# The down projection's leftover columns accumulated in the banks of the second segment's groups

## The reference, cut to what matters

```python
x = x + (x @ W.T + b + coeff * (x @ (2 * mask - 1)))        # stage 1, 8 x 256 tokens, 1024 wide
gate = x @ W_gate.T + 0.5 * (x @ A_gate[i].T) @ B_gate[i].T # F = 2752, i: adapter of the sequence, rank 16
up   = x @ W_up.T   + 0.5 * (x @ A_up[i].T)   @ B_up[i].T
act  = silu(gate) * up
x    = x + act @ W_down.T + 0.5 * (act @ A_down[i].T) @ B_down[i].T   # the stage of the change
```

## Time and profile before

| | |
|---|---|
| runs, median of 3 | 1665.02 us (1662.74 to 1666.45) |
| the profiled execution | 1666.28 us |
| its span, first to last instruction | 1664.6 us |
| TensorE busy | 1574.9 us (95%) |
| VectorE busy | 1247.0 us (75%) |
| ScalarE busy | 798.7 us (48%) |
| granted TensorE clock, mean | 0.981 |

### The profile page before, as it was taken

One profiled execution on the slowest core, in us unless ns is written; L12 is line 12 of the kernel. 1 busy time (PEld: TensorE's weight loads), 2 busy tenths in 40 slices (PEclk: granted clock), 3 DMA queues, 4 the chain that ended last, 5 costly groups with the idle time before them and its releaser, 6 DMA issues.

```text
span 1664.6 us, 22933 instructions
## 1 busy us (share of the span) xinstructions
PE 1574.9 (95%) x7502; PEld 1318.0 (79%) x7502; DVE 1247.0 (75%) x2168; ACT 798.7 (48%) x1466; POOL 331.7 (20%) x629
## 2 busy tenths in 40 slices
PE   6999958999999999998999769999999999999999
PEld 6999936888888888877888558888888888777887
DVE  7998767766666766679888786666667667698886
ACT  7998644444444444443333354444444444443332
POOL 0100121222222222232410010222222222402210
PEclk9999969999999999999999989999999999999999
DMA  8979572444444444694983643444444444968763
GB/s 328 347 285 309 177 246 86 149 149 149 141 149 138 147 143 142 219 332 162 362 272 106 202 137 114 148 149 149 148 149 149 149 147 144 339 193 283 252 208 117
DMA packets 135813, 321.03 MB, mean 193 GB/s; under 512 B 19344, under 2 KB 42000, under 8 KB 135696
## 3 DMA queue, kind: packets, MB, share of 16 engines
q0 software_dynamic: 55072, 175.81, 31.8%
q1 hardware_dynamic: 76016, 135.37, 24.6%
q10 hardware_dynamic: 4608, 8.39, 1.4%
HBM read 229.32 MB, written 90.18 MB: 192 GB/s over the span
## 4 chain that ended last, share of the span: by engine, by line
PE 84%; DVE 9%; DMA 4%; issue 2%; ACT 1%; SPq 1%; POOL 0%; DVEq 0%; ACTq 0%; POOLq 0%
PE ps L1321 57%; PE ps L1317 24%; DMA fx<-x_scratch 2%; PE ps L1423 2%; DVE acc L958 2%; DVE lo L955 2%; DVE op_b L955 1%; DVE fx L955 1%; DVE raw L955 1%; PE ps L1402 0%; DMA m_raw<-in_mask 0%; DVE m_raw L958 0%; DMA x_in<-in_x 0%; DMA a_in<-in_a_gu 0%; ACT hi L650 0%
## 5 line engine op out<-in xcount | busy, mean ns | idle before, releaser
L1321 PE MATMUL ps<-op_b,hi 128*128 128x512 f32 x1696 | 526.3, 392 | 17.4 <-ACT ps L650 9.8
L955 DVE TENSOR_TENSOR lo<-raw,hi 128x512 fp32r<-128x512 f32 (+2 forms) x646 | 339.0, 532 | 135.1 <-ACT hi L650 132.6
L650 ACT ACTIVATE hi<-raw 128x512 fp32r<-128x512 f32 (+1 forms) x598 | 308.8, 520 | 238.8 <-PE ps L1321 204.6
L1321 PEld LDWEIGHTS ps<-op_b,hi 128*128 128x128 f32 x1696 | 320.0, 189 | 87.6 <-ACT ps L650 10.7
L1321 PE MATMUL ps<-op_b,lo 128*128 128x512 f32 x848 | 332.4, 392 | 0.0
L1321 PE MATMUL ps<-op_d,hi 128*128 128x512 f32 x800 | 250.6, 395 | 11.8 <-DVE acc L958 11.8
L1317 PE MATMUL ps<-op_b,hi 128*128 128x512 f32 x720 | 227.3, 397 | 9.5 <-DVE op_b L955 9.5
L958 DVE TENSOR_TENSOR acc<-acc,ps 128x512 f32<-128x512 f32 x272 | 185.2, 686 | 54.9 <-PE ps L1321 51.5
L533 POOL DMA_DIRECT2D operand_scratch<-ot x140 | 75.6, 540 | 660.4 <-DVE ot L955 625.1
L1321 PEld LDWEIGHTS ps<-op_d,hi 128*128 128x128 f32 x800 | 150.6, 190 | 48.8 <-DVE acc L958 17.1
L1321 PEld LDWEIGHTS ps<-op_b,lo 128*128 128x128 f32 x848 | 160.2, 189 | 34.0
(11 more groups left out here) (123 smaller groups left out, 2204.2 us busy)
## 6 DMA issues: line engine op xcount, KB each, us to landing
operand_scratch<-ot POOLq DMA_DIRECT2D x140, 512.0 KB, 3.9
op_d<-operand_scratch POOLq DMA_DIRECT2D x140, 512.0 KB, 10.7
raw<-in_wgu SPq DMA_DIRECT2D x168, 256.0 KB, 4.2
m_raw<-in_mask SPq DMA_DIRECT2D x64, 512.0 KB, 5.7
raw<-in_wd SPq DMA_DIRECT2D x160, 128.0 KB, 5.0
fx<-x_scratch SPq DMA_DIRECT2D x64, 256.0 KB, 3.8
b_in<-in_b_gu POOLq DMA_DIRECT2D x264, 32.0 KB, 2.3
w_in<-in_w SPq DMA_DIRECT2D x16, 512.0 KB, 5.5
```

Source lines behind the costliest of these rows:

```text
L650: return nc.scalar.activation(o, i, ACT.Copy)
L955: return nc.vector.tensor_tensor(o, a, b, ALU.subtract)
L1321: return mm(dst, weight, v, start=False, stop=stop, skip_group_check=True)
```

## The change

The eight pieces move into segment 1, two into each group: the even one (h = 2 hp) ahead of p7, the odd one ahead of p4. Their halves accumulate onto the group's own banks: the even piece onto y and z, the first-listed half of the odd one into ps6 or ps7, its second half onto x. So p3's add of y comes after the even piece, and of the leftover's adds one a group remains (the bank ps6 or ps7). `bd_in` becomes two slots, each with the adapter rows of one group, in a place of its own; it is loaded four times a block. All of segment 1's operand loads are issued without waiting, and the next block's adapters are loaded after segment 2's operands.

The diff, its core (left out: declarations, `left_bank`, the same change of `bd_in`'s index on VectorE):

```diff
@@ -17,6 +17,7 @@
 SEGS, SEGK = 5, 2
+LEFT_SEG = 1
@@ -65,12 +66,12 @@
     for hp in range(HP):
-        order += [("d", s, seg, hp, u) for u in PRODUCTS[:6]]
-        if seg == 0 and hp == 0:
-            order += [("td", s, PAIRS)]
-        order += [("d", s, seg, hp, u) for u in PRODUCTS[6:]]
-    if seg == 0:
-        order += [("l", s, h) for h in range(HT)]
+        for u in PRODUCTS:
+            if u == "p4" and (seg, hp) == (0, 0):
+                order += [("td", s, PAIRS)]
+            if u in ("p7", "p4") and seg == LEFT_SEG:
+                order += [("l", s, 2 * hp + int(u == "p4"))]
+            order += [("d", s, seg, hp, u)]
     return order
@@ -227,15 +228,14 @@
     with ExitStack() as down:
-        with ExitStack() as before:
-            sb(before, "pad_bd", [P, 40 * 256], f32)
-            bd_in = sb(before, "bd_in", [P, 4, H], f32)
...
+        sb(down, "pad_lw", [P, LW_RING * HALVES, P], f32)
+        bd_in = sb(down, "bd_in", [P, 2, 4, 2 * P], f32)
@@ -520,9 +520,9 @@
                     weight_dma(("d", s, seg, hp), name)
-            if seg == 0:
-                for h in range(HT):
-                    weight_dma(("l", s, h), "a")
+                if seg == LEFT_SEG:
+                    for h in (2 * hp, 2 * hp + 1):
+                        weight_dma(("l", s, h), "a")
@@ -552,12 +552,15 @@
-    def load_b_down(adapter):
+    def load_b_down(adapter, s, hp):
+        if hp > 1:
+            pool.wait_ge(lo_ready, at["l", s, 2 * hp - 3] + 1)
...
-                pool.dma_start(bd_in[r:r + RANK, b, :], b_down[ds(adapter[b], 1), :, :].rearrange(
-                    "a r n -> (a r) n")).then_inc(bd_loaded, 16)
+                pool.dma_start(bd_in[r:r + RANK, hp % 2, b, :],
+                               b_down[ds(adapter[b], 1), :, 2 * P * hp:2 * P * (hp + 1)].rearrange(
+                                   "a r n -> (a r) n")).then_inc(bd_loaded[hp % 2], 16)
@@ -623,26 +626,29 @@
             load_acc(s, h)
-        load_b_down(adapter)
-        for u in ("p1", "p5", "p6", "p3", "p4"):
+        for u in PRODUCTS[:3]:
...
-        pool.wait_ge(lo_ready, at["l", s, HT - 1] + 1)
-        load_operand(s, 1, "p7")
-        load_operand(s, 1, "p2")
-        if s < BLOCKS - 1:
+        load_b_down(adapter, s, 0)
+        for u in PRODUCTS[3:]:
+            load_operand(s, 1, u)
+        load_b_down(adapter, s, 1)
+        for seg in range(2, SEGS):
+            for u in PRODUCTS:
+                pool.wait_ge(pe_done, done["d", s, seg - 2, HP - 1, u])
+                load_operand(s, seg, u)
+                if seg == 2 and u in ("p6", "p7"):
+                    load_b_down(adapter, s, 2 + int(u == "p7"))
+            if seg > 2 or s == BLOCKS - 1:
+                continue
...
+            pool.wait_ge(lo_ready, at["l", s, HT - 1] + 1)
...
-        for seg in range(2, SEGS):
-            for u in PRODUCTS:
-                pool.wait_ge(pe_done, done["d", s, seg - 2, HP - 1, u])
-                load_operand(s, seg, u)
@@ -723,9 +729,10 @@
             _, s, h = key
-            act.wait_ge(bd_loaded, 16 * 8 * (s + 1))
+            hp, cols = h // 2, slice(h % 2 * P, (h % 2 + 1) * P)
+            act.wait_ge(bd_loaded[hp % 2], 16 * 8 * bd_turn(s, hp))
...
-            copy(tile[TR:P, :, :], bd_in[TR:P, :, h * P:(h + 1) * P])
+            copy(tile[TR:P, :, :], bd_in[TR:P, hp % 2, :, cols])
@@ -1033,8 +1040,6 @@
     def make_first(g):
-        if g[0] == "l":
-            return
@@ -1074,7 +1080,7 @@
             sub(slot_ap(lo, key), src, slot_ap(hi, key)).then_inc(lo_ready, 1)
-        if n + 1 < len(plan.items) and plan.group(plan.items[n + 1]) != g:
+        if n + 1 < len(plan.items) and plan.items[n + 1][-1] in ("p1", "q1"):
@@ -1206,22 +1212,20 @@
             dve.wait_ge(acc_loaded[2 * hp + row], 16 * (s + 1))
-        dve.wait_ge(pe_done, done[key])
+        dve.wait_ge(pe_done, done["l", s, 2 * hp] if (seg, u) == (LEFT_SEG, "p3") else done[key])
...
-        if (seg, hp, u) == (1, 0, "p5"):
-            dve.wait_ge(left_added, left_count(s, HT - 1, HALVES - 1))
+        if (seg, u) == (LEFT_SEG + 1, "p5"):
+            dve.wait_ge(left_added, left_count(s, hp))
...
-    def add_left(key):
-        _, s, h = key
-        dve.wait_ge(pe_done, done[key])
-        for half in range(HALVES):
-            dst = acc[:, h, half * N:(half + 1) * N]
-            if h == 0 and half == 0:
-                dve.wait_ge(d_added, d_count(s, 0, HP - 1, "p4"))
-            add(dst, dst, left_bank(h, half)[:, :]).then_inc(left_added, 1)
+    def add_left(s, hp):
+        dve.wait_ge(pe_done, done["l", s, 2 * hp + 1])
+        dve.wait_ge(d_added, d_count(s, LEFT_SEG, hp, "p7"))
+        dst = acc[:, 2 * hp + 1, N:2 * N]
+        add(dst, dst, ps[6 + hp % 2][:, :]).then_inc(left_added, 1)
@@ -1272,10 +1276,14 @@
             evict(key)
-        elif key[0] == "d" and key[4] != "p1":
+        elif key[0] == "d" and key[4] != "p1" and (key[2], key[4]) != (LEFT_SEG, "p3"):
             add_down(key)
         elif key[0] == "l":
-            add_left(key)
+            _, s, h = key
+            if h % 2:
+                add_left(s, h // 2)
+            else:
+                add_down(("d", s, LEFT_SEG, h // 2, "p3"))
         if key[0] == "d" and key[2:] == (0, 0, "p1"):
@@ -1447,8 +1455,6 @@
             pe.wait_ge(c_made, c_count(s, PAIRS, "c12"))
-        if (seg, hp, u) == (1, 0, "p1"):
-            pe.wait_ge(left_added, left_count(s, HT - 2, HALVES - 1))
@@ -1461,29 +1467,29 @@
     def left(s, h):
-        key = ("l", s, h)
+        key, hp = ("l", s, h), h // 2
+        g = (s * SEGS + LEFT_SEG) * HP + hp
+        x_ps, y_ps, z_ps = ps[3 * (g % 2)], ps[3 * (g % 2) + 1], ps[3 * (g % 2) + 2]
...
-            pe.wait_ge(d_added, d_count(s, 0, HP - 2, "p4"))
-        elif h == 1:
-            pe.wait_ge(td_sum, 2 * HALVES * (s + 1))
-        elif h == 2:
-            pe.wait_ge(d_added, d_count(s, 0, HP - 1, "p4"))
-        else:
-            pe.wait_ge(left_added, left_count(s, h - 3, HALVES - 1))
+            pe.wait_ge(td_ready, 2 * HALVES * (s + 1))
...
-        for half in range(HALVES):
-            dst, i = left_bank(h, half), 2 * ot_slot[s, KP, ("b11", "b12")[half]]
-            mm(dst[:, :], high[:, 0:P], ot[:, i, :], start=True, stop=False)
-            mm(dst[:, :], high[:, 0:P], ot[:, i + 1, :], start=False, stop=False)
-            mm(dst[:, :], high[:, 2 * P:3 * P], ot[:, i, :], start=False, stop=False)
-            if h == 0 and half == 0:
-                pe.wait_ge(td_ready, 2 * HALVES * (s + 1))
-            mm(dst[:, :], high[:, P:2 * P], act21[:, half * N:(half + 1) * N], start=False, stop=False)
+        for half, dst in ((1, ps[6 + hp % 2] if h % 2 else y_ps), (0, x_ps if h % 2 else z_ps)):
+            mm_to = mm_new if h % 2 and half else mm_on
+            if h % 2 == 0 and half == 0:
+                pe.wait_ge(d_seeded, g + 1)
+            elif h % 2 and half == 0:
+                pe.wait_ge(d_added, d_count(s, LEFT_SEG, hp, "p7"))
+            elif h % 2 and hp > 1:
+                pe.wait_ge(left_added, left_count(s, hp - 2))
+            i = 2 * ot_slot[s, KP, ("b11", "b12")[half]]
+            mm_to(dst[:, :], high[:, 0:P], ot[:, i, :], start=h % 2 == 1 and half == 1)
+            mm_to(dst[:, :], high[:, 0:P], ot[:, i + 1, :])
+            mm_to(dst[:, :], high[:, 2 * P:3 * P], ot[:, i, :])
+            mm_to(dst[:, :], high[:, P:2 * P], act21[:, half * N:(half + 1) * N])
...
-                end = mm(dst[:, b * S:(b + 1) * S], low[:, v * P:(v + 1) * P], act_t[:, cols], start=False,
-                         stop=b == 1)
+                end = mm_to(dst[:, b * S:(b + 1) * S], low[:, v * P:(v + 1) * P], act_t[:, cols], stop=b == 1)
```

13 lines of the change are left out of this document (7 added, 6 removed).

## The result

The changed kernel took 1652.67 us (median of 4 runs, 1651.78 to 1655.76) against 1664.67 us of the kernel before (4 runs, 1662.74 to 1666.45): ratio 0.9931, 95% interval 0.9914 to 0.9949.

A forecast was written before the change was run, and what follows sets the result against it. VectorE was taken to bound the leftover, TensorE the rest of the down projection. -11.58 + 0.9 = -10.7 us took the profiled 1666.28 to 1655.6; the profiled run being 1.26 above the median, 1654.3 was predicted, range 1651.8 to 1661.3.

The forecast's parts named there:

- the sum's first term: Both blocks, segment 0's last group to segment 2: TensorE's gaps shrink by 5.77 and 5.81 us, together -11.58 us.
- the new wait: Segment 1, odd piece's second half waiting for p7's add, and p3: 0.15 us in 6 groups, 0.9 us; margin 0.14.
- The leftover's gaps: TensorE from segment 0's last group to segment 2: 6.58 us lost per block disappear, 0.81 at p3 remains.
- The term for p3 carried over: Segment 0's last group: p3 still starts late, as one group earlier, costing 0.81 us against 1.85 before.
- The adds: VectorE: 16 leftover adds per block become 4, freeing 7.2 us of VectorE per block, worth nothing by themselves.
- VectorE's queue in a group: Segment 1: VectorE needs 11.6 of 14.2 us per group; p7's add done at 11.3, p5's at 3.7.
- (1): Rival: VectorE's chains in segment 1 overrun in full, 6.9 us instead of 0.9, so 1660.3 us; chance 0.13.
- (2): Rival: VectorE becomes segment 1's bound, 16.7 against 14.2 us a group, 20 us in 8 groups: 1673.5 us; chance 0.05.
- (4): Rival: the gaps only move, 1.4 us in each of eight groups, no change, 1665 us; chance 0.07.
- (3): Rival: GpSimd's adapter issues in segment 1's first two groups hold VectorE, 5.2 us in both blocks: 1659.5 us; chance 0.05.
- Loads and adapters: Operand, b_down and next block's adapter loads, issued at new times, all arrive before they are needed: cost 0.
- One sign of being wrong: The prediction would be wrong if block 1 started later than its 5.8 us earlier.

The follow-up runs named there:

- the run with the first piece late: Kernel before, with the first leftover piece's weights prepared after p5's add of segment 0's last group instead of ahead of it: 1665.02 us, ratio 1.0002.
- the run with four adds in the old place: Kernel before, pieces still between segments 0 and 1, only 4 of 16 leftover adds per block, the other halves left out of the output: 1656.16 us.
- The experiment on the chain: Changed kernel plus two unread VectorE additions after p6's add in segment 1's groups 0 to 2, ahead of p7's add: 1659.61 us, ratio 0.9966.

## Why the prediction was right

**The whole.** The sum was -10.7 us. The two stretches together gave 11.5, the 11.58 of the sum's first term; the 0.9 for the new wait was not lost. That the two profiled executions differ by 10.5, so near to 10.7, is in part luck, since other parts of the program took 1 us back. The medians differ by 12.0.

**The leftover's gaps** (-6.58 + 0.81 per block). Right in cause and size: the stretch came out at 67.23 us, forecast 67.2. That the first piece's weights held up p3 is borne out by the run with the first piece late, where that wait is gone. The term for p3 carried over, 0.81, measured 0.87 and 0.83 (group of 10.39 and 10.35 us). It stayed when the leftover went to segment 2, so the prediction's cause fits, the steps of the adapter's input together with two sums.

**The adds** ("worth nothing by themselves once TensorE is the bound"). Too little said. It did the sum no harm, because the gaps were counted once, but the run with four adds in the old place shows 4.65 us per block from them alone: they would have made TensorE the bound there too. And with the pieces between products and on banks of their own they are still worth 1.2 us per block, which the sum had at nothing.

**VectorE's queue in a group.** The chain from p6 was forecast to end with p7's add at 11.3 us from the group's start and p5's add at 3.7. VectorE's timeline of the second group, which starts at 773.51:

```profile
776.49 0.68 DVE L965 TENSOR_TENSOR acc<-acc,ps 128x512 f32<-128x512 f32 x1
777.80 0.69 DVE L965 TENSOR_TENSOR acc<-acc,ps 128x512 f32<-128x512 f32 x1 [0.63 <-PE ps L1329]
778.89 0.89 DVE L962 TENSOR_TENSOR lo<-raw,hi 64x128 fp32r<-64x128 f32 x4 [0.40 <-ACT hi L656]
...
784.11 0.68 DVE L965 TENSOR_TENSOR acc<-acc,ps 128x512 f32<-128x512 f32 x1
...
786.54 0.69 DVE L965 TENSOR_TENSOR acc<-acc,ps 128x512 f32<-128x512 f32 x1 [0.81 <-PE ps L1329]
787.63 0.89 DVE L962 TENSOR_TENSOR lo<-raw,hi 64x128 fp32r<-64x128 f32 x4 [0.40 <-ACT hi L656]
```

p5's add ends at 777.17, 3.66 from the start; p7's at 784.79, 11.28. Adding up spacings instead of listed durations was what made that exact; in full durations it would have been 0.8 us more.

**The new wait** (0.9 us) is the term that was mis-sized. It measured 0: no group of segment 1 in the changed kernel lost over 0.02 us. The weight load for the half that waits started at 785.06, 11.55 from the start, where I had it wanted at 11.44, so the margin was 0.27 us and not 0.14. The experiment on the chain agrees with that figure: 1.2 us of extra work cost 0.97, which leaves 0.23. For the first group the prediction had 1.36 us more of room, and it has 0.57.

**Rivals.** The overrun (1) and the new bound (2) are excluded by segment 1's groups of 14.2 us; (2) came near only with twelve adds more per block, at 13.65 us of VectorE in a group, and even that cost 1.2 us per block and not 10. (4), that the gaps only move, is excluded by the 67.2 us. (3), that GpSimd holds VectorE up: in segment 2 GpSimd is busy 18.33 us now and was 7.39 before, and VectorE's own work there is 32.16 against 32.01 us, with one instruction more; the groups of segment 1 in which GpSimd issued the adapter loads (6.06 and 5.60 us busy) are no longer than the third (0.46). So the locked read interface of the Trainium skill's page SBUF — State Buffer ("Who interferes with whom") costs nothing here, in line with its remark, called inferred there, that issuing transfers needs the write interface.

**Loads and adapters** (0). As forecast, within a few us. GpSimd's timeline, block 0, where the earlier trace rows had the loads of segment 2 at 794.80:

```profile
750.74 1.10 POOL L569 DMA_DIRECT2D op_d<-operand_scratch  x2 [10.15 <-PE ps L1325]
...
784.02 2.02 POOL L561 DMA_DIRECT2D bd_in<-in_b_down  x4 [0.31 <-issue]
...
809.91 2.92 POOL L540 DMA_DIRECT2D a_in<-in_a_gu  x4 [21.73 <-DVE lo L962]
...
821.99 7.42 POOL L569 DMA_DIRECT2D op_d<-operand_scratch  x14 [0.56 <-PE ps L1329]
```

Segment 2's loads start at 750.74 (said: 751), the last of b_down ends at 786.0 (785), the adapters start at 809.91 (810), segment 3's loads at 821.99 (825). Segment 3 starts at 854.25 without a wait.

**One sign of being wrong came up.** Block 1 was not to start later than 5.8 us earlier. Its down projection starts 5.07 us earlier (1433.14 against 1438.21) and its last group of segment 0 4.93 (1469.00 against 1473.93). Block 0's gain of 5.73 is whole in its own stretch; the gate and up stage between the blocks took 1.84 us more and the start 1.35 less in that execution. A sign taken across 500 us of other work mixes in its variation; the length of the stretch itself doesn't.
